# Reordering the prologue of a two-layer attention and FFN kernel, with padding matmuls and a context split moved to GpSimd

## The chip, the core and the metric

The kernel runs on one NeuronCore of a Trainium2 chip. The core has TensorE (PE), VectorE (DVE), ScalarE (ACT), GpSimd (POOL) and SyncE (SP), which here only issues DMAs; each works through its own list of instructions and waits on semaphores for the others. The metric is the device time of one execution in microseconds, lower is better.

## The reference

Sixteen batches of 56 tokens with 128 features attend to a context of 1500 rows each. Cut to what matters:

```
x = x + L0_xattn(layernorm(x), ctx, ctx, Wq, bq, Wk, bk, Wv, bv, Wo)   # 16 heads of 8
x = x + L0_ffn(layernorm(x), w_gate, w_up, w_down)                     # quantised, 384 wide
x = x + L1_xattn(layernorm(x), ctx, ...)                               # slot attention, 3 rounds with a GRU
x = x + L1_ffn(layernorm(x), Wg, Wu, Wd)                               # 8 experts, 512 wide

# L0_xattn
q = (xq @ Wq.T + bq); k = (xk @ Wk.T + bk); v = (xv @ Wv.T + bv)       # split into heads
weights = softmax(q k.T * scale); out = (weights @ v) @ Wo.T
```

The change concerns the first lines only: the first layernorm, the queries, and what the first two batches need before the loop over batches begins.

## The kernel before

**Layout.** Everything is kept with the 128 features on the partitions. `xT` holds all 896 tokens side by side. The context of a batch (128 x 1500 numbers, 750 KB) is loaded into `ctx32` and split into two half-precision parts, `ctx_hi` (a cast) and `ctx_lo` (the difference), so that three half-precision matmuls replace one in single precision. The weights `wk` and `wv` are split in the same way by `split_weights` on DVE: two scaled casts, the scaled bias, two differences.

**The stages of a batch.** `keys` makes 500 columns of keys in three matmuls into PSUM bank `MISC`; ACT casts them to `k_hi` (`k_high`, L711), DVE makes the remainder `k_lo` (`k_low`, L927); there are three such parts, j = 0, 1, 2, and one buffer `k_lo` for all batches. SP copies `k_hi` and `k_lo` with twelve DMAs into `kstack` (`stack`). `values` makes four chunks of values in twelve matmuls (L1495), three times per batch, evacuated by ACT into `v_aug` (L719, L720). GpSimd spreads the queries over heads: `qdiag` (L563) for the maxima, `qstack` (L573) for the scores. `maxima` are 21 units per batch: PE multiplies `qdiag` and `k_hi` into one of two banks (L1508), DVE reduces 500 columns to one (L936). From these the shift of the softmax is taken (`shift_halves`, `shift`, `shift_rows`). Only then can `scores` of that batch go (L1525), twelve steps, each followed by an exponential on ACT (L702) and, every second step, by `weigh` (L1539, L1544).

**Order.** All engines follow an order written out by hand. In the loop `main`, PE interleaves step c of batch b with maxima, keys and values of the next batches; `AHEAD`, `PER_STEP`, `KEYS_AT` and `VALUES_AT` are its tables. Before it comes the prologue. There PE does: means of `xT` (L1461), variance (L1466), first keys (`first_keys`), spread of the reciprocal root over the partitions (L1472), second keys, the queries (L1559), third keys, the 21 maxima of batch 0 with the three value blocks at steps 7, 9 and 11 of `FIRST_STEPS`, the shift, and then keys and first maxima of batch 1. DVE centres (L911), splits the weights (L979 to L984), takes the reciprocal (L915), normalises (L921), takes `q_lo` (L991), casts `ident` (L995) and reduces. ACT casts the first context itself (`context_high`, L724), squares (L692), takes the square root (L697), casts queries (L734) and keys, issues eight of the twelve DMAs that replicate the queries into `q_rep` (L740), and casts the second context. The functions of ACT need tables; a change of table is an instruction of its own.

**Waits that matter.** `keys(b, 0)` waits for `ctx_split` (both parts of the context), for `constants` (the weights' parts) the first time, and for the values before it. The first maximum waits for `qdiag_built`, `k_hi_done` and `ready` at 7, which DVE gives after `ident`. `k_low` of a later batch waits until the DMAs have copied the `k_lo` before it. `scores` waits for the stack, `q_built` and `shift_done`.

## Time and profile before

| | us |
|---|---|
| median of 3 runs | 772.85 (771.12 to 773.10) |
| the profiled execution's own time | 772.33 |
| its span on the core | 770.5 |
| PE busy | 672.9 (87%) |
| DVE busy | 596.2 (77%) |
| ACT busy | 528.6 (69%) |
| GpSimd busy | 444.5 (58%) |

The span runs from the first to the last instruction; 1.8 us of the execution's time lie around it. Times in the text are microseconds from the start of the span. The loop over the batches starts at about 43 us and lasts until about 345 us; the prologue is what comes before it. The page's granted clock is TensorE's clock as a share of 2.4 GHz: it is either 1.00 or 0.50 (1.2 GHz), and a number in between is the mean of a stretch with both.

### The profile page before, as it was taken

The numbers are of one execution on the slowest core, as the hardware profiler recorded it, in microseconds if no ns is written. First come the engines' busy times: TensorE is split into PE (matmuls) and PEld (weight loads), VectorE is DVE, ScalarE is ACT, GpSimd is POOL, SyncE is SP. The second block draws the span as 40 slices with busy tenths as digits, with TensorE's granted clock in tenths as the row PEclk, the third lists the DMA queues.
The fourth block names the chain that finished last, engine by engine and source line by source line (L and its number), as shares of the span: only waits on it lengthen the run. The fifth ranks groups of instructions, "written<-read, shape, count | busy, mean of one in ns | idle before, by whom it ended". The sixth has DMA issues, their size and how long they took to land.

```text
span 770.5 us, 23878 instructions
## 1 busy us (share of the span) xinstructions
PE 672.9 (87%) x8894; PEld 485.5 (63%) x8894; DVE 596.2 (77%) x1122; ACT 528.6 (69%) x1153; POOL 444.5 (58%) x484
## 2 busy tenths in 40 slices
PE   5789999999999999997753868889888688899997
PEld 2257777777777777776531457778888677455553
DVE  3878887887777778888778456888888888858983
ACT  3266776767777677775463398999999984455554
POOL 1667777777777777771100033666776884466564
PEclk8799999999999999999885878999999989999999
DMA  6535444444444444331410501550555431002100
GB/s 191 156 96 174 131 134 121 114 132 140 140 140 130 132 128 133 95 104 20 147 50 0 228 21 64 198 213 28 183 215 186 164 137 63 12 1 83 42 0 25
DMA packets 26864, 86.16 MB, mean 112 GB/s; under 512 B 5844, under 2 KB 7764, under 8 KB 26788
## 3 DMA queue, kind: packets, MB, share of 16 engines
q1 hardware_dynamic: 26408, 84.73, 34.6%
q8 instruction: 46, 0.75, 0.4%
q10 hardware_dynamic: 384, 0.46, 0.2%
q14 instruction: 26, 0.21, 0.1%
HBM read 65.19 MB, written 0.46 MB: 85 GB/s over the span
## 4 chain that ended last, share of the span: by engine, by line
PE 62%; DVE 15%; ACT 15%; issue 3%; SPq 2%; POOL 2%; DMA 1%; DVEq 0%; ACTq 0%; POOLq 0%
PE ps L1508 9%; PE ps L1525 8%; PE ps L1539 8%; ACT c_prob L841 7%; PE ps L1495 5%; PE ps L1818 4%; PE ps L1820 4%; PE ps L1819 4%; PE ps L1766 3%; DVE tile_max L936 3%; PE ps L1484 3%; ACT w0T L841 2%; PE ps L1748 2%; PE ps L1544 2%; ACT merge_w L841 2%
## 5 line engine op out<-in xcount | busy, mean ns | idle before, releaser
L936 DVE TENSOR_REDUCE tile_max<-ps 128x1 f32<-128x500 f32 x336 | 215.2, 675 | 48.8 <-PE ps L1508 48.6
L702 ACT ACTIVATE probs<-ps 125x896 f32<-125x896 f32 x192 | 175.3, 916 | 92.7 <-PE ps L1525 91.8
L1508 PE MATMUL ps<-k_hi,qdiag 128*128 128x500 f16 x336 | 129.6, 387 | 6.7 <-DVE tile_max L936 2.8
L841 ACT ACTIVATE c_prob<-ps,c_bias,row_scale 125x56 f32<-125x56 f32 x384 | 118.8, 547 | 8.1 <-DVE c_bias L1240 8.1
L1525 PE MATMUL ps<-qstack,kstack 98*125 98x224 f16 x768 | 106.3, 261 | 0.4
L631 POOL TENSOR_TENSOR c_prob<-c_prob,c_weight 125x672 f32<-125x672 f32 x32 | 43.1, 1346 | 102.6 <-DVE c_weight L1254 102.5
L1525 PEld LDWEIGHTS ps<-qstack,kstack 98*125 98x125 f16 x768 | 85.8, 136 | 20.9 <-ACT probs L702 2.8
L676 POOL TENSOR_TENSOR ctx_lo<-ctx_hi,ctx_lo 128x448 f16<-128x448 f32 x62 | 64.6, 1042 | 52.1 <-ACT ctx_lo L877 52.1
L1748 PE MATMUL ps<-query_hi,ctx_hi 128*128 128x56 f16 x576 | 54.3, 193 | 29.0 <-ACT c_prob L841 21.0
L1539 PE MATMUL ps<-probs,v_aug 125*32 125x168 f32 x1536 | 74.8, 312 | 3.3 <-ACT probs L702 2.5
L573 POOL TENSOR_TENSOR qstack<-q_rep,slot_mask 96x224 f16<-96x224 f32 (+1 forms) x64 | 33.7, 556 | 74.6 <-PE ps L1525 69.3
L588 POOL TENSOR_TENSOR rows_in<-rows_in 125x768 f32<-125x768 f32 (+2 forms) x96 | 68.9, 717 | 7.5
L1748 PEld LDWEIGHTS ps<-query_hi,ctx_hi 128*128 128x128 f16 x576 | 48.5, 100 | 38.2 <-ACT c_prob L841 23.5
L1818 PE MATMUL ps<-ctx_lo 128*128 128x448 f16 x192 | 67.7, 353 | 3.2 <-DVE ctx_lo L1385 1.6
L1819 PE MATMUL ps<-ctx_lo 128*128 128x448 f16 x192 | 67.7, 352 | 0.0
L1820 PE MATMUL ps<-ctx_lo 128*128 128x448 f16 x192 | 67.7, 352 | 0.0
L872 ACT ACTIVATE ctx_hi<-ps 128x448 f32<-128x448 f32 x64 | 34.8, 543 | 45.5 <-PE ps L1820 45.4
L1539 PEld LDWEIGHTS ps<-probs,v_aug 125*32 125x32 f32 x1536 | 40.2, 109 | 31.8 <-issue 23.8
L1378 DVE SCALAR_TENSOR_TENSOR ctx_hi<-ctx_hi,ps 128x448 f32<-128x448 f32 x64 | 39.0, 614 | 25.7 <-ACT ctx_hi L872 25.4
L558 POOL TENSOR_TENSOR ctx_lo<-ctx,ctx_hi 128x1500 f32 (+1 forms) x16 | 48.6, 3035 | 11.3 <-ACT ctx_hi L724 9.1
L1748 PE MATMUL ps<-query_hi,ctx_lo 128*128 128x56 f16 x576 | 54.0, 192 | 0.0
L1748 PE MATMUL ps<-query_lo,ctx_hi 128*128 128x56 f16 x576 | 54.0, 192 | 0.0
(279 smaller groups left out, 1722.8 us busy)
## 6 DMA issues: line engine op xcount, KB each, us to landing
row_tiles<-in_ctx_rows_wide SPq DMA_DIRECT2D x40, 774.0 KB, 5.7
ctx<-in_ctxT SPq DMA_DIRECT2D x16, 750.0 KB, 5.3
rows_in<-in_ctx_rows SPq DMA_DIRECT2D x16, 750.0 KB
kstack<-k_hi SPq DMA_DIRECT2D x128, 93.8 KB, 2.7
kstack<-k_lo SPq DMA_DIRECT2D x64, 93.8 KB, 2.7
ctx_hi<-in_wg SPq DMA_DIRECT2D x8, 256.0 KB, 2.7
ctx_hi<-in_wu SPq DMA_DIRECT2D x8, 256.0 KB, 3.1
ctx_hi<-in_wd SPq DMA_DIRECT2D x8, 256.0 KB, 3.5
```

The source lines that it names most:

```text
L588: nc.gpsimd.tensor_tensor(a, a, z, ALU.add).then_inc(rows_step, 1)
L676: nc.gpsimd.tensor_tensor(hidden_lo[i], hidden[i], hidden_hi[i], ALU.subtract).then_inc(h_lo_done, 1)
L702: nc.scalar.activation(probs[c % RING_P][0:CH, :].rearrange("p (k w) -> p k w", k=2), score_tile(c)[0:CH], ACT.Exp, scale=float(HD) ** -0. ...
L841: last = nc.scalar.activation(c_prob[n % PROBS][:, c, :], ps[0:CH, 2 * (n % 2) + c // 6, bass.ts(c % 6, TOK)], ACT.Exp, bias=c_bias[n % 2] ...
L936: nc.vector.reduce_max(tile_max[:, u % MAXT, u // MAXT:u // MAXT + 1], ps[:, MAXB + (u + p) % 2, 0:KCOLS], AX.X).then_inc(max_done, 1)
L1508: nc.tensor.matmul(ps[:, MAXB + (u + p) % 2, 0:KCOLS], qdiag[p][:, bass.ts(t, 128)], k_hi[p][:, bass.ts(j, KCOLS)], start=True, stop=True) ...
L1525: last = nc.tensor.matmul(ps[0:CH, 2 * (c % 2) + g // 2, bass.ts(g % 2, GW)], kstack[p][0:STACK_ROWS, g, bass.ts(c, CH)], qstack[p][0:STAC ...
L1539: nc.tensor.matmul(ps[GR * g:GR * g + GR, OUTB, 0:three], v_aug[p][0:CH, of, g, HD:], probs[of % RING_P][0:CH, GW * g:GW * g + three], sta ...
L1748: last = nc.tensor.matmul(ps[:, 2 * (n % 2) + c // 6, bass.ts(c % 6, TOK)], l, r, start=(j == 0), stop=(j == 2))
L1818: nc.tensor.matmul(bank, w1_hi[w][:, at], x_high, start=first, stop=False)
L1819: nc.tensor.matmul(bank, w1_lo[w][:, at], x_high, start=False, stop=False)
L1820: return nc.tensor.matmul(bank, w1_hi[w][:, at], x_low, start=False, stop=last)
```

## The change

1. DVE clears a tile `warm` right at its start, and PE issues matmuls on it whose results nobody reads (`warm_up`, 512 columns each): 10 before the means, 5 between means and variance, 8 between variance and spread.
2. ACT no longer casts the first two contexts; GpSimd does both parts. ACT loads the square root's table at its start instead of at the root.
3. PE does no keys between variance and spread, and only the first keys before the queries; the second come after them, and the third after the first two maxima. DVE splits the weights after the reciprocal instead of before it.
4. GpSimd splits the second context before it spreads the stacked queries, not after.
5. ACT puts the third key's cast between the two groups of four DMAs that replicate the queries.
6. The values of batch 0 come at steps 2, 4 and 6 of the first maxima. `keys(1, 0)` and its cast come at step 9.
7. After the shift, PE does `keys(1, 1)`, then the scores of steps 0 and 1 around the first maximum of batch 1; ACT's first two exponentials follow directly. `main(0, 0)` leaves both out.

The diff, cut to its core:

```diff
-        FIRST_VALUES = {7: 0, 9: 1, 11: 2}
+        FIRST_VALUES = {2: 0, 4: 1, 6: 2}
+        KEY_AHEAD = 9
@@ gpsimd
-                if not (isinstance(b, int) and b < 2):
-                    pool.wait_ge(ctx_loaded[p], landed(b, p, 1))
-                    nc.gpsimd.tensor_copy(ctx_hi[:, b, :], ctx32[:]).then_inc(ctx_split_hi, 1)
+                pool.wait_ge(ctx_loaded[p], landed(b, p, 1))
+                nc.gpsimd.tensor_copy(ctx_hi[:, b, :], ctx32[:]).then_inc(ctx_split_hi, 1)
...
             plain_queries(0, 0)
+            split(1, 1)
             pool.wait_ge(q_rep_loaded, 16 * 3 * GROUPS)
             stacked_queries(0, 0)
-            split(1, 1)
             plain_queries(1, 1)
@@ scalar
-            context_high(0)
+            act.wait_ge(ready, 1)
+            load_table(ACT.Sqrt)
             act.wait_ge(ready, 3)
             layernorm_sd(0)
             act.wait_ge(constants, 1)
             k_high(0, 0, 0)
-            k_high(0, 0, 1)
...
-            k_high(0, 0, 2)
+            k_high(0, 0, 1)
             act.wait_ge(q_hi_done, 2)
             for r in range(2):
+                if r:
+                    k_high(0, 0, 2)
                 for g in range(GROUPS):
                     nc.scalar.dma_start(q_rep[GR * r:GR * (r + 1), g, :], q_hi[GR * g:GR * (g + 1), :]).then_inc(q_rep_loaded, 16)
-            context_high(1)
             for c in range(NCH):
                 if c in FIRST_VALUES:
                     v_evacuate(0, 0, FIRST_VALUES[c])
+                if c == KEY_AHEAD:
+                    k_high(1, 1, 0)
                 if c == NCH - 1:
                     load_table(ACT.Exp)
-            k_high(1, 1, 0)
             k_high(1, 1, 1)
+            exp(0, 0)
+            exp(0, 1)
@@ vector
             nc.vector.memset(eps_ln[:], LN_EPS).then_inc(ready, 1)
+            nc.vector.memset(warm[:], 0.0).then_inc(magic_ready, 1)
...
-            layernorm(0, split_weights, lambda: k_low(0, 0, 0))
-            k_low(0, 0, 1)
+            layernorm(0, None, split_weights)
+            k_low(0, 0, 0)
...
-            k_low(0, 0, 2)
+            k_low(0, 0, 1)
             dve.wait_ge(params, PARAMS)
             nc.vector.tensor_copy(ident[:], ident32[:]).then_inc(ready, 1)
             for c in range(NCH):
                 maxima(0, 0, step_units(FIRST_STEPS, c))
+                if c == 0:
+                    k_low(0, 0, 2)
...
+            k_low(1, 1, 0)
             shift_rows(0, 0)
-            k_low(1, 1, 0)
-            maxima(1, 1, range(1))
             k_low(1, 1, 1)
-            maxima(1, 1, range(1, UNITS_AHEAD))
+            maxima(1, 1, range(UNITS_AHEAD))
@@ tensor
+            def warm_up(n):
+
+                for _ in range(n):
+                    nc.tensor.matmul(ps[:, MAXB + 1, 0:512], warm[:, 0:128], warm[:], start=True, stop=True)
+
+            pe.wait_ge(magic_ready, 1)
+            warm_up(10)
             pe.wait_ge(first_params, 16 * len(first_list))
-            layernorm(0, None, first_keys)
-            keys(0, 1)
+            layernorm(0, lambda: warm_up(5), lambda: warm_up(8))
+            pe.wait_ge(constants, 1)
+            keys(0, 0)
...
-            keys(0, 2)
+            keys(0, 1)
...
                 maxima(0, 0, second)
+                if c == 0:
+                    keys(0, 2)
+                if c == KEY_AHEAD:
+                    keys(1, 0)
                 if c == NCH - 1:
                     shift(0, 0)
-            keys(1, 0)
+            keys(1, 1)
+            scores(0, 0, 0)
             maxima(1, 1, range(1))
-            keys(1, 1)
+            scores(0, 0, 1)
             maxima(1, 1, range(1, UNITS_AHEAD))
```

On DVE, from the centring to the first maxima (`out_raw` is the memory of the early weights, of the normalised x and of `q_lo`). Before:

```order
L911 TENSOR_TENSOR probs<-xT,ps 128x448 [waits ln_mean,first_params]
L911 TENSOR_TENSOR probs<-xT,ps 128x448 [waits ln_mean]
L979 TENSOR_SCALAR wk_hi<-out_raw 128x128 [waits k_params]
L984 SCALAR_TENSOR_TENSOR wv_lo<-out_raw,wv_hi 128x128
L915 RECIPROCAL rstd<-sd 128x224 [waits ln_sd]
L927 SCALAR_TENSOR_TENSOR k_lo<-ps,bk_scaled,k_hi 128x500 [waits k_hi_done]
L921 TENSOR_TENSOR out_raw<-probs,ps 128x448 [waits ln_spread] x2
L995 CAST ident<-ident 128x128 [waits params]
L936 TENSOR_REDUCE tile_max<-ps 128x1 [waits max_ready] x21
```

Now:

```order
L913 TENSOR_TENSOR probs<-xT,ps 128x448 [waits ln_mean,first_params]
L913 TENSOR_TENSOR probs<-xT,ps 128x448 [waits ln_mean]
L917 RECIPROCAL rstd<-sd 128x224 [waits ln_sd]
L982 TENSOR_SCALAR wk_hi<-out_raw 128x128 [waits k_params]
L987 SCALAR_TENSOR_TENSOR wv_lo<-out_raw,wv_hi 128x128
L923 TENSOR_TENSOR out_raw<-probs,ps 128x448 [waits ln_spread] x2
L998 CAST ident<-ident 128x128 [waits params]
L938 TENSOR_REDUCE tile_max<-ps 128x1 [waits max_ready] x2
L929 SCALAR_TENSOR_TENSOR k_lo<-ps,bk_scaled,k_hi 128x500 [waits k_hi_done]
L938 TENSOR_REDUCE tile_max<-ps 128x1 [waits max_ready] x19
```

The five instructions of the splits (two shown) moved behind the reciprocal, and one `k_lo` went in among the reductions.

On GpSimd, from its start to the spreading of the second batch's queries. Before:

```order
L558 TENSOR_TENSOR ctx_lo<-ctx,ctx_hi 128x1500 [waits ctx_split_hi]
L563 TENSOR_TENSOR qdiag<-q_hi,head_mask 128x896 [waits q_hi_done,params]
L573 TENSOR_TENSOR qstack<-q_rep,slot_mask 96x224 [waits q_rep_loaded]
L573 TENSOR_TENSOR qstack<-q_rep,slot_mask 96x224 x3
L558 TENSOR_TENSOR ctx_lo<-ctx,ctx_hi 128x1500 [waits ctx_split_hi]
```

Now:

```order
L557 CAST ctx_hi<-ctx 128x1500 [waits ctx_loaded0]
L559 TENSOR_TENSOR ctx_lo<-ctx,ctx_hi 128x1500 [waits ctx_split_hi]
L564 TENSOR_TENSOR qdiag<-q_hi,head_mask 128x896 [waits q_hi_done,params]
L557 CAST ctx_hi<-ctx 128x1500 [waits ctx_loaded1]
L559 TENSOR_TENSOR ctx_lo<-ctx,ctx_hi 128x1500 [waits ctx_split_hi]
L574 TENSOR_TENSOR qstack<-q_rep,slot_mask 96x224 [waits q_rep_loaded]
```

Both casts came to this engine, and the second context follows `qdiag` directly.

On PE, from the shift of batch 0 into the loop. Before:

```order
L1515 MATMUL ps<-ident,neg_pair 2x128 [waits pair_done]
L1484 MATMUL ps<-ctx_hi,wk_hi 128x500 [waits v_done,ctx_split]
L1508 MATMUL ps<-k_hi,qdiag 128x500 [waits k_hi_done,qdiag_built,max_done]
L1484 MATMUL ps<-ctx_hi,wk_hi 128x500 [waits k_lo_done]
L1508 MATMUL ps<-k_hi,qdiag 128x500 [waits shift_done,max_done]
L1525 MATMUL ps<-qstack,kstack 125x224 [waits shift_done,q_built,stack_loaded0]
L1508 MATMUL ps<-k_hi,qdiag 128x500 [waits max_done] x2
L1525 MATMUL ps<-qstack,kstack 125x224 x4
```

Now:

```order
L1488 MATMUL ps<-ctx_hi,wk_hi 128x500 [waits v_done,ctx_split]
L1512 MATMUL ps<-k_hi,qdiag 128x500 [waits max_done]
L1519 MATMUL ps<-ident,neg_pair 2x128 [waits pair_done]
L1488 MATMUL ps<-ctx_hi,wk_hi 128x500 [waits k_lo_done]
L1529 MATMUL ps<-qstack,kstack 125x224 [waits shift_done,q_built,stack_loaded0]
L1512 MATMUL ps<-k_hi,qdiag 128x500 [waits k_hi_done,qdiag_built,max_done]
L1529 MATMUL ps<-qstack,kstack 125x224 x4
L1512 MATMUL ps<-k_hi,qdiag 128x500 [waits shift_done,max_done]
```

The first keys of batch 1 moved ahead of the last maximum and the shift, and the first two scores ahead of all but one of batch 1's maxima.

## Rows read from the trace of the kernel before

**Rows 1.** Busy time by stretch: stretch, its length, each engine's busy time, PEclk, DMA

```profile
100.00:200.00 100.00, 97.94 (x1512) 71.89 (x1511) 80.93 (x142) 70.89 (x102) 74.49 (x70) 1.00 0.45 131
```

**Rows 2.** The chain that ended last, in order of time: start, us, what

```profile
9.93 3.03 POOL ctx_lo L558
...
14.50 3.04 PE ps L1472 x8
...
20.27 0.82 PE ps L1484 x3
...
21.11 0.69 ACT k_hi L711
21.82 0.74 DVE k_lo L927
...
32.56 1.28 PE ps L1495 x12
...
36.00 0.71 PE ps L1495 x12
...
39.06 1.28 ACT L684
```

**Rows 3.** Busy time by stretch, in the prologue; the third number from the right is PEclk

```profile
5.00:8.60 3.60, 3.29 (x4) 1.18 (x4) 0.70 (x2) 0.19 (x1) 0.00 (x0) 1.00 0.95 298
...
14.30:17.60 3.30, 3.30 (x10) 2.71 (x10) 1.38 (x3) 0.68 (x1) 0.00 (x0) 0.50 0.65 250
...
25.30:32.00 6.70, 5.83 (x11) 0.98 (x11) 6.59 (x11) 1.44 (x1) 4.00 (x5) 0.50 0.73 179
```

**Rows 4.** Matmuls of two lines: duration in ns min/median/max, first and last start

```profile
L1461 PE MATMUL ps<-xT,ones_mean x4: 891/954/1116, 5.2 to 7.6; 128*128 128x448 f32 x4
...
L1559 PE MATMUL ps<-out_raw x4: 539/539/540, 18.6 to 19.7; 128*128 128x448 f32 x4
```

**Rows 5.** Timeline, 8 to 23 us: start, us, engine, line, instruction, idle before

```profile
8.41 1.44 ACT L724 CAST ctx_hi<-ctx 128x1500 f16<-128x1500 f32 x1 [6.39 <-DMA ctx<-in_ctxT]
...
9.06 0.22 DVE L979 TENSOR_SCALAR wk_hi<-out_raw 128x128 f16<-128x128 f32 x1
...
9.76 1.04 ACT L692 ACTIVATE probs<-probs 128x448 f32<-128x448 f32 x2
...
10.81 1.28 ACT L697 ACT_TABLE_LOAD   x1
...
12.58 1.55 DVE L915 RECIPROCAL rstd<-sd 128x224 f32<-128x224 f32 x1 [2.64 <-ACT sd L697]
...
17.58 0.62 DVE L921 TENSOR_TENSOR out_raw<-probs,ps 128x448 f32<-128x448 f32 x1 [0.87 <-PE ps L1472]
...
19.52 1.39 ACT L734 ACTIVATE q_hi<-ps,bias_qkv 128x448 f16<-128x448 f32 x2
...
21.05 1.69 POOL L563 TENSOR_TENSOR qdiag<-q_hi,head_mask 128x896 f16<-128x896 f16 x1 [8.10 <-ACT q_hi L734]
...
21.12 5.28 ACTq L740 DMA_DIRECT2D q_rep<-q_hi  x8
...
22.48 0.34 DVE L995 CAST ident<-ident 128x128 f16<-128x128 f32 x1
```

**Rows 6.** Timelines of DVE and of GpSimd in a later stage, 638 to 640 us

```profile
638.79 1.02 DVE L1338 TENSOR_SCALAR rs_y<-rs_var 128x112 int32<-128x112 int32 x1
...
638.05 1.69 POOL L631 TENSOR_TENSOR merge_w<-merge_w,c_weight 125x672 f32<-125x672 f32 x1 [1.21 <-DVE c_weight L1254]
639.82 1.49 POOL L641 TENSOR_SCALAR ctx_lo<-ctx_hi 128x512 f16<-128x512 f32 x1
```

**Rows 7.** Timeline of DVE: the 21 reductions of batch 0

```profile
23.30 9.98 DVE L936 TENSOR_REDUCE tile_max<-ps 128x1 f32<-128x500 f32 x15 [0.48 <-PE ps L1508]
34.29 3.91 DVE L936 TENSOR_REDUCE tile_max<-ps 128x1 f32<-128x500 f32 x6 [1.02 <-PE ps L1508]
```

**Rows 8.** Timeline: the first and the third exponential of batch 0 on ACT

```profile
43.60 0.92 ACT L702 ACTIVATE probs<-ps 125x896 f32<-125x896 f32 x1
...
47.72 0.92 ACT L702 ACTIVATE probs<-ps 125x896 f32<-125x896 f32 x1
```

More of the change, by code:

```diff
@@ L720, in v_evacuate @@
                 nc.scalar.activation(dst[:, :, 0:HD], src[:, :, GR - HD:], ACT.Copy, scale=1.0 / W_SCALE).then_inc(v_done, 1)
-            def context_high(b):
-                act.wait_ge(ctx_loaded[b], 16)
-                nc.scalar.copy(ctx_hi[:, b, :], ctx32[:]).then_inc(ctx_split_hi, 1)
-            context_high(0)
+            act.wait_ge(ready, 1)
+            load_table(ACT.Sqrt)
             act.wait_ge(ready, 3)
```

20 lines of the change are left out of this document (10 added, 10 removed).

## The prediction

> **What bounds the kernel now.** I read the busy time by stretch first. Between 100 and 200 us, in the loop over the batches, PE is busy 97.94 us of 100 [rows 1]: this stage is a queue of PE work, so whatever comes before it moves its end by the same amount, and a head start is neither lost nor multiplied. The change touches only what lies before that loop, the first 46 us. Every gain has to be found there, and I follow it to the third exponential of batch 0 (47.72 us), after which both kernels issue the same instructions in the same order.
>
> Second, the chain of waits. It comes through the first context's load, ACT's cast, GpSimd's subtraction up to 12.96 us [rows 2], the queries, 21 reductions on DVE, and a table load of 1.28 us on ACT in front of the second batch's first key. Third, the granted clock of TensorE [rows 3]. It is 0.50 from 14.3 to 17.6 and from 25.3 to 32.0, the second being a stretch in which PE issues one matmul per reduction. The record says 1.00 from 5.0 to 8.6, but there the durations contradict it: the mean's matmuls take 954 ns a record and the queries', of the same shape, 539 ns [rows 4]. So the means also ran at 1.2 GHz, and the engine was idle before them.
>
> **Part 1, normalisation.** Before, ACT casts the context (1.44 us), then squares from 9.76, then loads a table from 10.81 (1.28 us), and the reciprocal starts at 12.58 [rows 5]. Afterwards GpSimd does the cast, which costs it about the same, so its subtraction still ends near 12.96. The table is loaded during the first DMA wait, the squares follow the centring at once, and the reciprocal starts between 9.3 and 10.7, depending on how early the 10 + 5 + 8 padding matmuls lift the clock. Even the late end leaves the reciprocal's end (1.55 us long) before 12.96. So the early chain is not worth its own 2 to 3 us: it runs into GpSimd.
>
> It runs into it twice. `keys(0, 0)`, which now stands ahead of the queries on PE, needs `ctx_lo`, as it did. And DVE's splits of the weights, five instructions of which the first starts at 9.06 and takes 0.22 us [rows 5], move from a time at which GpSimd had not begun to one in which it subtracts. The row at 638.79 shows what this does: an elementwise DVE instruction on 112 columns takes 1.02 us, beginning while GpSimd works from 638.05 for 1.69 us, and ends 0.07 us behind it, just as GpSimd's next begins at 639.82 [rows 6]. I take it that the splits wait until 12.96 and then take their 0.9 us (9.06 to about 9.94 before), to 13.9. The Trainium skill, "SBUF — State Buffer", section "Who interferes with whom", says that a VectorE instruction with two SBUF inputs, or in a two-port mode, and a GpSimd instruction that reads SBUF exclude each other for the whole instruction. By that rule, which speaks against this order of the splits, the trace agrees; without it term 1 would be the better end of its bounds, below.
>
> The two halves of the normalised x (0.62 us each, the last at 17.58 before [rows 5]) then end at 15.1, where they ended at 18.20. From there to the end of the second `q_hi` it was 2.71 us (to 20.91), of which some 0.3 was PE finishing key matmuls; now 2.4, to 17.5. **Term 1: -3.4 us.** The normalised halves count here because they queue behind the splits on DVE. Bounds: if the splits are not held up, `keys(0, 0)` is what remains and this is 1.2 us better (-4.6); if the queries run at 1.2 GHz (their four records at 0.95 instead of 0.54 [rows 4], less overlap), 1.0 worse.
>
> From `q_hi` to the first reduction it was 2.39 us (20.91 to 23.30): `qdiag` on GpSimd beside key cast, `k_lo` and `ident` [rows 5, 7]. The same instructions stand there now, with the second key in the third's place: 0. But `ident` took 0.34 us and ended as `qdiag` did, 22.8: it too was held by GpSimd. Now GpSimd goes straight on with the second context's cast and subtraction (1.43 and 3.02 us). `ident` is due 0.2 us before `qdiag` ends, and gets its turn between the two. Bounds: 0 to +4.5, on which the rivals below turn.
>
> **Part 2, the maxima.** 21 reductions took 14.9 us, 23.30 to 38.20: 9.98 us for 15, 3.91 for 6, and one stall of 1.02 [rows 7]. The third key is now inside. DVE has `k_lo` there (0.74, some 0.7 pipelined [rows 2]), and waits about 0.5 for it, because ACT issues four of its eight query DMAs (5.28 us for eight [rows 5]) before it gets to that key's cast. **Term 2: +1.2 us.** The row on ACT's second context cast leaves for GpSimd, which has the slack.
>
> The stall comes from `values`: its twelve matmuls take 1.28 us at half clock against 0.71 at full [rows 2]; with one matmul for the next reduction behind them that is more than the one reduction that DVE has in hand. Before, the first block met the half clock and the other two the full one. Now the blocks stand at steps 2, 4 and 6, just after 5 us in which PE has almost nothing (two maxima, a key), which is what it did before the fall at 25.3. I expect the first block surely and the second about as likely as not at half clock: 1.5 stalls for one. **Term 3: +0.5 us** (0 stalls -1.0, 3 stalls +2.0). The last reduction then ends at 36.5 instead of 38.2.
>
> **Part 3, into the loop.** Call the last reduction's end E. Before, shift, `keys(1, 0)`, table load and its key cast followed, the first exponential came at E + 5.4 and the third at E + 9.5 [rows 8]. Now `keys(1, 0)` and its cast lie before E and the table load beside shift and shift copy. After E: shift values 0.6, `k_lo` 0.74, shift copy 0.63, `keys(1, 1)` from E + 1.45 for 0.82, its cast 0.69, so the first exponential at E + 3.0, a gain of 2.4. This doesn't last: the second batch's seven reductions before the third exponential begin after `k_lo` at E + 3.75 and take 7 x 0.665 = 4.7 us, so its scores come behind the seventh matmul at about E + 7.4, and the third exponential at E + 8.0. **Term 4: -1.5 us.** What is late next is DVE, not ACT. The copies of the second batch's key are ready with `k_lo`, nearly as much sooner. If the clock is at half again here (PE is sparse in the last seven reductions), the key's matmuls, the scores and the first loop steps cost 1.0 to 1.2 more; I give that 4 in 10. **Term 5: +0.4 us.**
>
> The memset of the padding's operand (under 0.5 us of DVE) lies in the DMA wait, and the 10 padding matmuls end before or up to 0.3 us after the data arrive: nothing, as that path has room up to 12.96.
>
> **The sum:** -3.4 + 1.2 + 0.5 - 1.5 + 0.4 = -2.8 us on the profiled execution's 772.33 us, which is 0.5 us under the median of 772.85: 769.5 us.
>
> **Rivals.**
> (a) Full clock throughout: no stall of the maxima and none in the loop's start, -1.5 - 0.4 on the sum: -4.7, 767.6 us. For it: the padding keeps PE dense up to 10.7. Against it: nothing pads PE after the queries.
> (b) The splits are not held: -4.0, 768.3 us. Against it is the row at 638.79.
> (c) `ident` arrives after GpSimd has gone on to the second context's cast and waits for that alone: +1.4, so 770.9 us. It needs a second key 0.2 us late, which half clock in the queries gives.
> (d) Slower: the same, but GpSimd passes from cast to subtraction without letting DVE in, so that `ident`, and with it the first maximum (which waits for `ready`), comes 4.5 us later. It decides from the moment that `ident` is issued behind `qdiag`'s end: -2.8 + 4.5 = +1.7, 774.0 us. Against it: at 639.8 DVE did get in between two.
> (e) The padding, all zeros, does not lift the clock. Then 23 matmuls stand in front for nothing: the variance waits for five (at 0.42 each), the spread for part of eight and itself runs at half clock (3.04 us [rows 2]), and `q_hi` ends at 20.1 to 23. With the middle of these, 20.7, term 1 is about 0 and the whole -0.2 to +0.6: 772.3 us. The Trainium skill, "TensorE: Matmul & The Clock Gate", Part 1, says that activity releases the throttle, and that all-zero operands do not trip another, current-driven limiter; by it padding of zeros should count. No row here has such matmuls.
>
> **How the numbers follow.** The forecast (-1.6 to -4.0) has 0.56, (a) 0.12, (b) 0.08, (c) 0.10, (d) 0.05, (e) 0.09. Leaving out (d) and the far end of (a), the range is 767.8 to 772.2 us. About 0.3%, 2.3 us, is what a measurement of this kernel can tell from no change. The forecast's middle lies only 0.5 beyond it, so two thirds of it count as faster, all of (a) and (b), and little else: faster 0.57. Slower by over 0.3% needs (d) with a second stall, or a worse (e): 0.05. The same: 0.38.
>
> **What would show it.** In the profile after: the variance's reciprocal well before 12.9, but the first split of the weights lasting until GpSimd's subtraction ends (if it takes 0.22, term 1 is larger); the first reduction near 19.9; `ident` ending within 0.1 us of `qdiag`; a gap of DVE near 1.0 us behind the first `values`, perhaps the second; the last reduction at 36 to 37; the third exponential 8 us behind it, and the rest of the execution as before, shifted. The prediction is wrong if the subtraction of the first context no longer ends near 13, if the maxima run without stalls, or if the clock in later stages falls elsewhere by chance and moves the end by more than the prologue does.

## The result, and the profile after the change

The changed kernel takes 770.66 us (median of 22 executions, 765.50 to 773.86), the kernel before 772.91 us beside it (22 executions): the ratio is 0.996, 95% interval 0.9945 to 0.9974. The ratios in this document are the estimates on record from the fast executions, not quotients of the medians beside them (here that would be 0.9971). The profiled execution took 771.68 us with a span of 769.8 us. Lines have moved a little against the rows of before: L702 is now L703, L936 is L938, L1484 is L1488, L1508 is L1512.

The prologue first. GpSimd's timeline (start, us, engine, line, instruction, idle before and its releaser):

```profile
9.02 1.43 POOL L557 CAST ctx_hi<-ctx 128x1500 f16<-128x1500 f32 x1 [8.20 <-DMA ctx<-in_ctxT]
10.54 3.03 POOL L559 TENSOR_TENSOR ctx_lo<-ctx,ctx_hi 128x1500 f16<-128x1500 f32 x1
...
19.65 1.43 POOL L557 CAST ctx_hi<-ctx 128x1500 f16<-128x1500 f32 x1
```

DVE's timeline of the same kernel, 9 to 21 us:

```profile
9.73 1.55 DVE L917 RECIPROCAL rstd<-sd 128x224 f32<-128x224 f32 x1 [1.80 <-ACT sd L698]
11.20 2.45 DVE L982 TENSOR_SCALAR wk_hi<-out_raw 128x128 f16<-128x128 f32 x1
...
14.23 1.15 DVE L923 TENSOR_TENSOR out_raw<-probs,ps 128x448 f32<-128x448 f32 x2
...
19.24 0.55 DVE L998 CAST ident<-ident 128x128 f16<-128x128 f32 x1
20.27 1.26 DVE L938 TENSOR_REDUCE tile_max<-ps 128x1 f32<-128x500 f32 x2 [0.48 <-PE ps L1512]
```

PE's timeline, the means, the spread and the first key:

```profile
5.50 1.77 PE L1465 MATMUL ps<-xT,ones_mean 128*128 128x448 f32 x4 [0.48 <-DMA spread<-in_spread]
...
11.34 1.78 PE L1476 MATMUL ps<-rstd,spread 128*128 128x224 f32 x8 [0.32 <-DVE rstd L917]
14.37 0.39 PE L1488 MATMUL ps<-ctx_hi,wk_hi 128*128 128x500 f16 x1 [1.25 <-DVE wv_lo L987]
```

Against [rows 2, 5]: the four means take 1.77 us instead of 3.29 and the spread 1.78 instead of 3.25 (3.04 on the chain of [rows 2]), so both run at 2.4 GHz. The reciprocal starts at 9.73 instead of 12.58. Then the first split lasts 2.45 us instead of 0.22 and ends at 13.65, 0.08 us behind GpSimd's subtraction. `ident` ends at 19.79, between `qdiag` and GpSimd's next instruction.

The maxima and the way into the loop, DVE's timeline:

```profile
21.82 0.74 DVE L929 SCALAR_TENSOR_TENSOR k_lo<-ps,bk_scaled,k_hi 128x500 f16<-128x500 f32 x1 [0.29 <-ACT k_hi L712]
22.48 2.04 DVE L938 TENSOR_REDUCE tile_max<-ps 128x1 f32<-128x500 f32 x3
25.54 2.64 DVE L938 TENSOR_REDUCE tile_max<-ps 128x1 f32<-128x500 f32 x4 [1.02 <-PE ps L1512]
28.77 2.43 DVE L938 TENSOR_REDUCE tile_max<-ps 128x1 f32<-128x500 f32 x4 [0.59 <-PE ps L1512]
31.41 4.19 DVE L938 TENSOR_REDUCE tile_max<-ps 128x1 f32<-128x500 f32 x7 [0.21 <-PE ps L1512]
36.38 0.68 DVE L938 TENSOR_REDUCE tile_max<-ps 128x1 f32<-128x500 f32 x1 [0.77 <-PE ps L1512]
```

The first and the third exponential, ACT's timeline:

```profile
40.79 0.92 ACT L703 ACTIVATE probs<-ps 125x896 f32<-125x896 f32 x1
...
45.72 0.92 ACT L703 ACTIVATE probs<-ps 125x896 f32<-125x896 f32 x1
```

Busy time by stretch; the third number from the right is the granted clock:

```profile
22.00:28.00 6.00, 4.62 (x26) 2.70 (x26) 4.76 (x8) 0.66 (x2) 2.18 (x1) 0.50 0.79 201
28.00:30.00 2.00, 1.32 (x10) 0.55 (x9) 1.41 (x4) 0.66 (x2) 1.79 (x4) 0.97 0.53 133
...
36.00:40.00 4.00, 2.60 (x13) 1.29 (x13) 2.48 (x6) 2.12 (x3) 3.92 (x3) 0.50 0.00 0
```

Where [rows 7] have one stall of DVE behind `values`, there are four, 2.59 us together: one at half clock (1.02), one in whose block of values the clock rises (0.59), one at full (0.21), and one of 0.77 us ahead of the last reduction, which is `keys(1, 0)`: its three matmuls take 0.37, 0.58 and 0.62 us, as the clock falls in the middle of them. The last reduction ends at 37.06 instead of 38.20. The clock is at 0.50 again from 36 to 40 us, and the third exponential comes at 45.72 instead of 47.72 [rows 8]: 2.00 us sooner, though the first context landed 0.6 us later in this execution (9.02 against 8.41).

Those 2.00 us don't arrive at the end. The copies of the shifted queries mark each batch on DVE (before, then after):

```profile
102.29 0.63 DVE L953 COPY qstack<-ps 2x896 f16<-2x896 f16 x1 [0.64 <-PE ps L1515]
...
143.59 0.63 DVE L953 COPY qstack<-ps 2x896 f16<-2x896 f16 x1 [0.64 <-PE ps L1515]
```

```profile
100.23 0.63 DVE L955 COPY qstack<-ps 2x896 f16<-2x896 f16 x1 [0.64 <-PE ps L1519]
...
141.70 0.63 DVE L955 COPY qstack<-ps 2x896 f16<-2x896 f16 x1 [0.65 <-PE ps L1519]
```

Two batches, one turn of the loop, take 41.30 us before and 41.47 after. Of the five turns from here to 307.40 us four take 41.46 to 41.48 us, where before all take 41.24 to 41.30; at the last copy (349.27 against 348.07) the lead is 1.20 us. On PE, after the change, the first scores of these four turns stand behind an idle of 0.24 to 0.32 us for which the profile names no releaser (issue); before has none there:

```profile
123.75 0.59 PE L1529 MATMUL ps<-qstack,kstack 98*125 98x224 f16 x4 [0.24 <-issue]
```

This table gives such marks for every profile, so that what was drawn by chance (when the context lands) stands apart from what the kernel does. Context: start of its first cast. Queries and maxima: end of the second `q_hi` and start of the first reduction, behind the context. Block: from the first reduction to the end of the 21st. Start: from there to the third exponential. Loop: from there to the last (sixteenth) copy of the shifted queries. Rest: from there to the span's end. All in us; the ratio is that to before. `after_again` is the changed kernel once more: it was run to see whether the loss per turn belonged to one execution. It doesn't: most turns take 41.45 to 41.50 us again.

| kernel | context | queries | maxima | block | start | loop | rest | ratio (95%) |
|---|---|---|---|---|---|---|---|---|
| before | 8.41 | 12.50 | 14.89 | 14.90 | 9.52 | 301.55 | 421.23 | |
| changed | 9.02 | 8.85 | 11.25 | 16.79 | 8.66 | 302.35 | 421.73 | 0.996 (0.9945 to 0.9974) |
| after_again | 8.77 | 8.85 | 11.24 | 16.20 | 7.67 | 302.39 | 420.63 | 0.9936 (0.9909 to 0.9964) |
| splits_early | 8.51 | 11.75 | 14.14 | 14.57 | 7.67 | 302.41 | 425.40 | 1.0009 (0.9984 to 1.0034) |
| splits_early_again | 9.05 | 12.81 | 15.21 | 16.78 | 8.67 | 302.47 | 421.62 | |
| no_padding | 9.12 | 10.66 | 13.05 | 16.21 | 7.67 | 301.50 | 420.95 | 0.9964 (0.9933 to 0.9995) |
| values_later | 9.23 | 8.84 | 11.24 | 16.54 | 7.67 | 302.55 | 420.27 | 0.9958 (0.9928 to 0.9988) |
| pad_maxima | 9.47 | 10.09 | 12.48 | 14.62 | 7.67 | 302.31 | 417.75 | 0.9893 (0.9839 to 0.9946) |
| pad_maxima_again | 9.82 | 8.86 | 11.25 | 14.62 | 8.77 | 302.01 | 417.33 | 0.9923 (0.9899 to 0.9947) |
| pad_both | 8.57 | 8.84 | 11.24 | 14.62 | 7.66 | 301.75 | 421.06 | 0.9907 (0.9884 to 0.993) |
| shift_code | 7.90 | 9.08 | 11.60 | 15.39 | 7.67 | 301.57 | 420.57 | 0.9923 (0.9901 to 0.9945) |
| ident_late | 8.76 | 8.91 | 12.67 | 16.28 | 7.67 | 302.52 | 417.50 | |
| queries_first | 8.75 | 10.46 | 14.23 | 15.83 | 7.67 | 302.49 | 420.13 | 0.9975 (0.9954 to 0.9997) |
| loop_start_old | 7.79 | 8.85 | 11.24 | 14.52 | 12.67 | 302.35 | 422.63 | 0.998 (0.9953 to 1.0006) |

### The profile page after: what moved, and what is told of

It is laid out like the page before. It is cut to its first block, busy times and chain, and to the rows that moved or that the text cites. A ratio compares the mean times of both kernels' runs of the same rounds, so it can differ in the third digit from the quotient of the medians.

```text
span 769.8 us, 23925 instructions
## 1 busy us (share of the span) xinstructions
PE 675.6 (88%) x8917; PEld 487.0 (63%) x8917; DVE 597.5 (78%) x1123; ACT 525.1 (68%) x1151; POOL 447.1 (58%) x486
## 4 chain that ended last, share of the span: by engine, by line
PE 62%; DVE 16%; ACT 14%; issue 3%; SPq 2%; POOL 1%; DMA 1%; DVEq 0%; ACTq 0%; POOLq 0%
PE ps L1512 10%; PE ps L1529 9%; PE ps L1543 8%; ACT c_prob L843 7%; PE ps L1499 5%; PE ps L1832 4%; PE ps L1834 4%; PE ps L1833 4%; PE ps L1780 4%; PE ps L1488 3%; DVE tile_max L938 3%; ACT w0T L843 2%; PE ps L1762 2%; PE ps L1548 2%; ACT merge_w L843 2%
## 5 line engine op out<-in xcount | busy, mean ns | idle before, releaser
L938 DVE TENSOR_REDUCE tile_max<-ps 128x1 f32<-128x500 f32 x336 | 214.5, 675 | 51.3 <-PE ps L1512 51.0
L703 ACT ACTIVATE probs<-ps 125x896 f32<-125x896 f32 x192 | 175.3, 916 | 93.0 <-PE ps L1529 92.1
L1512 PE MATMUL ps<-k_hi,qdiag 128*128 128x500 f16 x336 | 128.4, 384 | 6.5 <-DVE tile_max L938 4.4
L1529 PEld LDWEIGHTS ps<-qstack,kstack 98*125 98x125 f16 x768 | 86.5, 137 | 22.3 <-ACT probs L703 3.7
L1241 DVE TENSOR_REDUCE ps<-ps 125x12 f32<-125x672 f32 x48 | 41.2, 859 | 15.9 <-PE ps L1762 15.8
```

Source lines behind the costliest of these rows:

```text
L703: nc.scalar.activation(probs[c % RING_P][0:CH, :].rearrange("p (k w) -> p k w", k=2), score_tile(c)[0:CH], ACT.Exp, scale=float(HD) ** -0. ...
L938: nc.vector.reduce_max(tile_max[:, u % MAXT, u // MAXT:u // MAXT + 1], ps[:, MAXB + (u + p) % 2, 0:KCOLS], AX.X).then_inc(max_done, 1)
L1512: nc.tensor.matmul(ps[:, MAXB + (u + p) % 2, 0:KCOLS], qdiag[p][:, bass.ts(t, 128)], k_hi[p][:, bass.ts(j, KCOLS)], start=True, stop=True) ...
L1529: last = nc.tensor.matmul(ps[0:CH, 2 * (c % 2) + g // 2, bass.ts(g % 2, GW)], kstack[p][0:STACK_ROWS, g, bass.ts(c, CH)], qstack[p][0:STAC ...
```

## The experiments

**Are the splits held by GpSimd, and can they get away from it?**

```
-            layernorm(0, None, split_weights)
+            layernorm(0, split_weights, None)
```

> The changed kernel, with the splits of the weights put back ahead of the variance's reciprocal on VectorE, where they stood before; all else stays. Theory (the splits were held for GpSimd's 3.03 us subtraction of the first context, the first split taking 2.45 us instead of 0.22): the splits now run between the centring and the reciprocal, beside GpSimd's cast rather than its subtraction, and take 0.9 us in all; the reciprocal may be held in their place but it is one instruction and its successors pass through PE; keys(0, 0) waits for GpSimd's subtraction alone, and the second q_hi ends 0.6 to 1.0 us sooner after the context has landed (9.0 instead of 9.7 us), third exponential and end -0.6 to -1.0 us. Rival (the lock only hands its wait to the next instruction on VectorE: the reciprocal or the normalised halves are held until the subtraction ends instead): second q_hi as in the changed kernel or up to 1.5 us later, end 0 to +1.5 us.

> The variant splits_early once more. Theory A (its 3.5 us over the changed kernel come from a fall of the clock at 362 to 369 us, by which its output projection and scores take 2.4 us longer, and more behind 400 us; the program makes it, as the ten executions at 774 us suggest): granted clock under 0.8 between 360 and 370 us again, end near 774. Theory B (that fall is a matter of chance): 1.00 between 360 and 370 us, end 770 to 772. The first splits of the weights take over 2 us in either, held by GpSimd's subtraction.

Measured: 774.19 us (10 executions; before 772.53), and 775.61 us for the second profile's execution. My theory got the cause right (GpSimd holds the splits) and the remedy wrong. DVE in the second profile, and GpSimd beside it:

```profile
9.80 0.76 DVE L982 TENSOR_SCALAR wk_hi<-out_raw 128x128 f16<-128x128 f32 x1 [1.50 <-DMA bias_qkv<-in_bias_qkv]
...
10.73 3.00 DVE L986 SCALAR_TENSOR_TENSOR wk_lo<-out_raw,wk_hi 128x128 f16<-128x128 f32 x1
...
13.86 1.54 DVE L917 RECIPROCAL rstd<-sd 128x224 f32<-128x224 f32 x1
```

```profile
10.56 3.02 POOL L559 TENSOR_TENSOR ctx_lo<-ctx,ctx_hi 128x1500 f16<-128x1500 f32 x1
```

The weights land at 9.80 us, when GpSimd is already in its cast. The first split ends 0.08 us behind that cast, the fourth waits out the whole subtraction (3.00 us instead of 0.29). From the context's landing to 13.6 us there is no gap of GpSimd's for them, and now the reciprocal queues behind them: it starts at 13.86 instead of 9.73, and the queries end 2.9 and 4.0 us later than in the changed kernel. That is the rival of the first expectation, at a higher price than its 1.5 us; 1.5 us of the 4.0 are the spread, which ran at half clock in the second profile (3.26 us instead of 1.78). Before, ACT did the cast, so GpSimd was still idle when the splits ran. By the rule of the Trainium skill, "SBUF — State Buffer", section "Who interferes with whom" (a VectorE instruction with two SBUF inputs or in a two-port mode and a GpSimd instruction that reads SBUF exclude each other), the traces agree: in eleven profiles a split starts before the subtraction's end and lasts until then, 0.6 to 3.0 us; in the first one of pad_maxima it starts behind it and takes 0.16 us. The reciprocal, with one input, ran beside GpSimd in its usual 1.55 us.

Of the second expectation, theory B holds for the clock: it was granted in full between 360 and 370 us this time, where the first profile had 0.70 (360 to 365) and 0.62 (365 to 370). Its time doesn't hold: 775.61 us instead of 770 to 772. In the first profile the late queries were repaid in the maxima (block 14.57 us, full clock) and lost again behind 345 us (rest of 425.40); in the second they weren't repaid. So the fall at 362 us isn't made by the program. That the slow median of ten comes from the prologue is likely, not shown: of the two profiles only the second is slow for that reason.

**What is the padding worth?**

```
-            warm_up(10)
+            warm_up(0)
...
-            layernorm(0, lambda: warm_up(5), lambda: warm_up(8))
+            layernorm(0)
```

> The changed kernel without its 23 matmuls of zeros; all else stays. Theory (the padding lifts the clock, as the means' 443 ns a record against 954 before suggests): means at 0.95 us a record, the variance later by about 1.5 us, still ahead of GpSimd's subtraction; spread and queries wholly or partly at half clock, second q_hi 0.5 to 1.5 us later after the context has landed (10.2 to 11.2 instead of 9.7 us), and the stalls behind the values as in the changed kernel: end +0.5 to +1.5 us. Rival (the path is pinned by GpSimd's subtraction and the held splits, so the clock ahead of it is worth nothing): second q_hi within 0.3 us of the changed kernel's and end within 0.3 us.

Measured: 770.74 us, ratio 0.9964, the same as the changed kernel's. PE's timeline:

```profile
5.89 3.32 PE L1465 MATMUL ps<-xT,ones_mean 128*128 128x448 f32 x4 [5.89 <-DMA spread<-in_spread]
...
13.27 3.35 PE L1476 MATMUL ps<-rstd,spread 128*128 128x224 f32 x8 [2.15 <-DVE rstd L917]
```

Matmuls of zeros do lift the clock: without them the means and the spread run at half of it, and the queries end 1.81 us later (10.66 against 8.85). The theory's part on the clock holds; its +0.5 to +1.5 us at the end don't come, and part of the reason is in the table: the loop is 0.85 us shorter than with the padding. Padding in the prologue is also no certain remedy: of the ten profiles with 10 matmuls of zeros at the start, the means took 1.77 us in seven, 2.47 in one and 3.35 in two (splits_early, queries_first). That led to the next run.

**Why do the turns of the loop take longer?**

```
-            warm_up(10)
+            warm_up(14)
```

> The changed kernel with 14 instead of 10 matmuls of zeros at the start, in the wait for the first DMAs; all else stays. It moves TensorE's instructions of the loop over the batches by four matmuls. In the loop the changed kernel and the two variants with as many matmuls ahead of the loop (splits_early, values_later) show an idle of 0.24 to 0.26 us put down to issue at the start of each turn, and lose 0.17 us per turn against before, 1.2 us in all; before, no_padding (23 fewer) and pad_maxima (20 more) don't. Theory (it depends on where the loop lies in the instruction memory, hence on the number of matmuls ahead): with four more the idle may stay or go, but it is the same in every turn, and it stands apart from the clock and from the prologue's times. Rival (it depends on the phase in which the loop is entered or on what another engine does in it): the idle stands as in the changed kernel, with copies of the shifted queries 41.4 us apart per turn. In both the prologue is that of the changed kernel within 0.5 us.

Measured: 767.41 us (2 executions, before 774.08). PE's first turn and DVE's copies:

```profile
120.50 0.59 PE L1529 MATMUL ps<-qstack,kstack 98*125 98x224 f16 x4 [0.19 <-issue]
```

```profile
138.47 0.63 DVE L955 COPY qstack<-ps 2x896 f16<-2x896 f16 x1 [0.64 <-PE ps L1519]
...
179.71 0.63 DVE L955 COPY qstack<-ps 2x896 f16<-2x896 f16 x1 [0.64 <-PE ps L1519]
```

The idle stands in the first turn alone; the next takes 41.24 us, and the loop 301.57 us as before, with the same instructions in it. So the rival (the idle stays as it was) is refuted, and the theory holds but for its "the same in every turn". (The expectation's 1.2 us in all is too much: the loop's difference is 0.80.) All eight profiles of kernels with 23 matmuls of zeros have the longer loop (302.35 to 302.55), those with 0 (before, no_padding) and 27 don't (301.50 to 301.57), and none of the three with 41 has the idle (their loops take 301.75 to 302.31 us, by longer first batches, which I haven't followed up). What is shown is that the number of matmuls ahead of the loop matters. Why is argued: what differs is where the loop's instructions lie. A load of instructions from memory isn't it: the trace lists packets of kind "instruction" on the DMA queues, and none of them moves between 130 and 330 us, where three of the four idles stand (206.5, 248.0 and 289.5 us). A phase in which the loop is entered is unlikely, since the third exponential comes between 43.88 and 49.71 us in the eight and the idle is there in all; and the other engines' programs are the same in the changed kernel and in shift_code.

**The values' place in the maxima.**

```
-        FIRST_VALUES = {2: 0, 4: 1, 6: 2}
+        FIRST_VALUES = {5: 0, 7: 1, 9: 2}
```

> The changed kernel with the three blocks of the first batch's values at steps 5, 7 and 9 of the maxima instead of 2, 4 and 6; all else stays. Theory (a block stalls VectorE by what its twelve matmuls take at half clock over at full, and what counts is how dense the blocks follow): the first block meets the half clock (stall near 1.0), the second and third as now (0.6 and 0.2), but the denser end lifts the clock for keys(1, 0), so that the 0.77 us stall ahead of the last reduction goes; last reduction 0 to 0.8 us sooner, third exponential up to 1.5 us sooner, end -0.3 to -1.5 us. Rival (the position doesn't matter, the stalls only move): the stalls' sum stays within 0.3 us of 2.59 and the end within 0.3 us.

Measured: 769.52 us, ratio 0.9958. DVE's timeline:

```profile
29.40 2.44 DVE L938 TENSOR_REDUCE tile_max<-ps 128x1 f32<-128x500 f32 x4 [1.00 <-PE ps L1512]
...
36.33 0.68 DVE L938 TENSOR_REDUCE tile_max<-ps 128x1 f32<-128x500 f32 x1 [0.95 <-PE ps L1512]
```

PE's timeline, ahead of the last reduction:

```profile
34.29 0.37 PE L1512 MATMUL ps<-k_hi,qdiag 128*128 128x500 f16 x1
35.29 0.37 PE L1488 MATMUL ps<-ctx_hi,wk_hi 128*128 128x500 f16 x1 [0.63 <-ACT v_aug L721]
```

The stalls are 1.00, 0.21, 0.21 and 0.95 us, 2.37 in all, instead of 2.59 and, in the second profile of the changed kernel, 2.01. By its number the rival holds, but the position does matter. The first block met the half clock again, because the clock fell later in this execution (at 25.8 us instead of 21.3). The last stall isn't one of the clock, which was granted in full from 29.2 us on: the edit puts the third block of values and `keys(1, 0)` into the same step, and the key's matmuls wait 0.63 us until ACT has evacuated that block. So this run doesn't test what a denser end is worth; one with the key a step later would. The end can't tell either: 0.9958 and 0.996 are the same within their intervals.

**The clock in the maxima.** Matmuls of zeros into a bank that is free there (18 more; the expectation's 20 is a slip of mine):

```
+            warm_up(7, 2)
             pe.wait_ge(ready, 7)
...
+                if c == 1:
+                    warm_up(3, 2)
+                if 7 <= c < KEY_AHEAD:
+                    warm_up(2, 2)
...
+                if c == KEY_AHEAD + 1:
+                    warm_up(4, 2)
```

> The changed kernel with 20 more matmuls of zeros, into a bank of PSUM that nothing else uses then: 7 ahead of the first maximum, 3 behind step 1, 2 behind each of steps 7 and 8, 4 behind step 10. Theory (the half clock is what makes the stalls of 1.02, 0.59, 0.21 and 0.77 us in the maxima and costs some 0.7 us at the loop's start): granted clock 1.00 through 20 to 42 us, stalls together under 0.8 us instead of 2.59, third exponential 8.0 instead of 8.66 us behind the last reduction; end -2 to -3 us. Rival (the padding stands in front of the maxima's own matmuls and only turns one stall into another, or the clock falls all the same): stalls together over 2 us and end -0.5 to +1.0 us.

> The variant pad_maxima once more, for its time and a second profile (it has 18 more matmuls of zeros than the changed kernel, not 20 as its first expectation says). Theory (full clock through the maxima and no idle in the loop's turns, 2.2 us and 1.2 us): stalls together under 1 us, third exponential 7.7 us behind the last reduction, ratio to before 0.990 to 0.995. Rival (its -6 us were for the most part a good draw behind 345 us): the maxima as said, ratio 0.995 to 0.998.

and, with 14 at the start, 6 ahead of the first maximum and 2 at each of the other places:

> Like pad_maxima with as many matmuls of zeros in all (41), spread otherwise: 14 instead of 10 at the start, so that they reach to 6.5 us and the wait for the spread's DMA (it landed between 5.2 and 7.4 us) finds TensorE busy; 6 ahead of the first maximum, 2 behind steps 1, 7, 8 and 10. Theory (a late spread DMA lets the clock fall before the means, which cost pad_maxima 0.7 and splits_early 1.6 us there; a longer padding closes it): means at 1.77 us for four records, second q_hi 8.9 us behind the context, maxima at full clock: 0 to -1.2 us against pad_maxima. Rival (fewer matmuls of zeros in the maxima let the clock fall there): stalls over 2 us, +1 to +2 us.

Measured: pad_maxima 766.33 and 766.07 us (before 772.53 and 772.92), pad_both 765.59 us, where the changed kernel beside it took 768.43. Stretches and reductions of pad_both:

```profile
22.00:28.00 6.00, 3.88 (x32) 2.16 (x32) 5.57 (x11) 1.32 (x4) 1.73 (x1) 1.00 0.75 181
...
36.00:40.00 4.00, 2.79 (x16) 1.32 (x14) 3.05 (x6) 2.29 (x3) 3.92 (x3) 1.00 0.01 2
```

```profile
24.07 2.43 DVE L938 TENSOR_REDUCE tile_max<-ps 128x1 f32<-128x500 f32 x4 [0.21 <-PE ps L1512]
...
33.75 0.68 DVE L938 TENSOR_REDUCE tile_max<-ps 128x1 f32<-128x500 f32 x1 [0.15 <-PE ps L1512]
```

For the maxima the theory holds in all three profiles: granted clock 1.00, stalls 0.21 three times and 0.15, a block of 14.62 us instead of 16.79 and 16.20. The full clock came without padding too, by itself, in splits_early and loop_start_old (blocks of 14.57 and 14.52 us), so part of this could be a draw; three out of three, and three medians below the changed kernel's two, speak against it. At the loop's start the theory holds in two of three: in pad_maxima_again the clock fell at 42 us, behind the last padding, and the start took 8.77 us. The reductions also come closer, 2.43 us for four where 9.98 for 15 [rows 7] stood mostly at half clock. One reduction lasts 0.67 to 0.68 us in both; but at full clock the next starts 0.59 us behind it, in before at half clock 0.67 to 0.70. There TensorE's record for a unit lasts 0.60 us instead of 0.38, and it waits for the bank that a reduction frees; so the likely reading is that the reductions wait for TensorE, in waits too short for the view to list. Of pad_maxima's 6 us over before, though, 3.5 to 3.9 lie behind 345 us (rest of 417.75 and 417.33 against 421.23), which pad_both's profile doesn't have: that part can't be put down to the padding. In pad_maxima the wait for the spread's DMA let the clock fall before the means once (2.47 us for four instead of 1.77); with 14 at the start they took 1.67 us in both kernels that have them. Against pad_maxima pad_both gained 0.5 us by the medians, which is within what was forecast and within the noise. pad_both is the version to keep: ratio 0.9907, 95% interval 0.9884 to 0.993, which lies wholly below the changed kernel's first interval and overlaps its second (0.9909 to 0.9964).

**Does `ident` wait once or twice?** A reciprocal of 112 columns that nothing reads delays it:

```
             dve.wait_ge(params, PARAMS)
+            nc.vector.reciprocal(rstd[:, 0:WIDE[0] // 4], sd[:, 0:WIDE[0] // 4])
             nc.vector.tensor_copy(ident[:], ident32[:]).then_inc(ready, 1)
```

> The changed kernel with one more instruction on VectorE (a reciprocal of 112 columns that nothing reads, about 0.8 us) just ahead of the cast of ident; all else stays. The cast now arrives some 0.4 us after GpSimd has gone on from qdiag to the cast of the second context (19.65 to 21.08 in the changed kernel). Theory of one wait (rival (c) of the prediction: VectorE gets in at the next boundary between two GpSimd instructions): ident ends as that cast does, near 21.2, and the first reduction starts 1.4 us later than in the changed kernel. Theory of two waits (rival (d): GpSimd keeps the port through cast and subtraction): ident ends near 24.2, the first reduction is 4.4 us later. No lock at all: +0.8.

Measured: DVE, and GpSimd's instruction behind the cast that ended at 20.87:

```profile
19.79 1.17 DVE L999 CAST ident<-ident 128x128 f16<-128x128 f32 x1
```

```profile
20.95 3.02 POOL L559 TENSOR_TENSOR ctx_lo<-ctx,ctx_hi 128x1500 f16<-128x1500 f32 x1
```

Where nothing holds it, as in queries_first, this cast takes 0.22 us. Here `ident` ends at 20.96, as the cast has ended (20.87) and the subtraction begins, and the maxima start 1.42 to 1.43 us later behind the context (12.67 against 11.25 and 11.24). One wait: the mechanism of (c), at its price of 1.4 us; (d) is refuted. The single execution took 767.19 us, no slower than the changed kernel: its rest is 417.50 us.

**Are the queries the path, or the keys?** The splits and `ident` go behind the normalised halves, the queries ahead of the first key on PE and ACT:

```
-            layernorm(0, None, split_weights)
-            k_low(0, 0, 0)
+            layernorm(0)
+            split_weights()
...
-            pe.wait_ge(constants, 1)
-            keys(0, 0)
             pe.wait_ge(ln_out, 2)
...
+            pe.wait_ge(constants, 1)
+            keys(0, 0)
             keys(0, 1)
```

> The changed kernel with the splits of the weights moved behind the two halves of the normalised x on VectorE (and ident's cast right behind them), the queries ahead of the first key on TensorE and ScalarE; all else stays. Theory (what term 1 stands on: the queries were late only because they queued behind splits that waited for GpSimd): the normalised halves end 0.8 us behind the spread's matmuls, the second q_hi ends 1.0 to 1.7 us sooner after the context has landed (7.2 to 7.9 us behind it instead of 8.85), the splits take 0.9 us as GpSimd has ended, the first reduction is 0.7 to 1.3 us sooner, the end -0.5 to -1.3 us. Rival (the key path, splits to first key to k_lo, is as long: what the queries gain the keys lose): first reduction within 0.3 us, end within 0.3 us. Second rival (clock: a head start given back by a longer half clock in the maxima, as splits_early's 2.4 us were repaid there): the last reduction within 0.3 us though the first is sooner.

Measured: 771.00 us, ratio 0.9975. DVE's timeline:

```profile
16.63 0.22 DVE L982 TENSOR_SCALAR wk_hi<-out_raw 128x128 f16<-128x128 f32 x1
...
22.32 0.74 DVE L929 SCALAR_TENSOR_TENSOR k_lo<-ps,bk_scaled,k_hi 128x500 f16<-128x500 f32 x1 [1.61 <-ACT k_hi L712]
```

Behind GpSimd's end a split takes 0.22 us again. But `k_lo` of the second key is now what the first reduction waits for: 3.77 us behind the queries instead of 2.40. In this execution the means ran at half clock (3.35 us), which spoils the comparison behind the context; counted from the spread's end (16.05; 13.12 in the changed kernel) the first reduction comes 6.93 us later instead of 7.15. The first rival holds for the first reduction: what the queries gain, the keys lose (0.22 us are left). The ends, 0.9975 and 0.996, can't be told apart.

**The way into the loop.** The prediction's part 3 undone: `keys(1, 0)` behind the shift, the first two scores and the order of `k_lo` and shift as before. PE's part of the edit (ACT and DVE follow it):

```
-                if c == KEY_AHEAD:
-                    keys(1, 0)
...
-            keys(1, 1)
-            scores(0, 0, 0)
+            keys(1, 0)
             maxima(1, 1, range(1))
-            scores(0, 0, 1)
+            keys(1, 1)
             maxima(1, 1, range(1, UNITS_AHEAD))
```

> The changed kernel with the way into the loop put back as before: the second batch's first key behind the shift instead of at step 9 of the maxima, the table of the exponential and the scores of the first two steps in the old order. Theory (term 4 of the prediction: this part is worth 1.5 us at equal clock): third exponential 9.5 us behind the last reduction at full clock, 10.5 at half, instead of 7.67 and 8.66; the stall of 0.77 us ahead of the last reduction is gone, as keys(1, 0) no longer stands there: together +1.0 to +1.5 us at the loop's start. Rival (the part is worth nothing, as VectorE's seven reductions of the second batch pace the start either way): third exponential within 0.3 us of the changed kernel's.

Measured: 773.00 us, ratio 0.998. A stretch and the third exponential:

```profile
33.00:44.00 11.00, 8.25 (x28) 3.74 (x29) 6.29 (x13) 2.70 (x4) 10.20 (x6) 0.50 0.22 75
```

```profile
46.22 0.92 ACT L703 ACTIVATE probs<-ps 125x896 f32<-125x896 f32 x1 [0.30 <-PE ps L1527]
```

The stall ahead of the last reduction is gone, and the block takes 14.52 us at full clock. Then the clock is at half for all of 11 us, and the third exponential comes 12.67 us behind them: 3.15 us more than before had at full clock (9.52), 4.0 to 5.0 more than the changed kernel. The rival is refuted, and the theory was right in its direction and too small: it had 10.5 us at half clock. The old order costs 1.85 us more at full clock (9.52 in before against 7.67), and 4.0 more at half (12.67 against 8.66); that it has more of TensorE's work for a half clock to stretch is my reading, not tested.

## Why the prediction was right, and where it was not

Forecast 769.5 us, range 767.8 to 772.2, measured 770.66. Some of this nearness is luck. The sum of -2.8 us was set on one profiled execution (772.33); set on the median of 772.85 it gives 770.05. Behind the context the two profiles of the changed kernel gained 2.61 and 4.20 us up to the third exponential, on average 0.6 more than forecast, and the loop, which the sum put at nothing, gave 0.8 back: two errors of opposite sign. By the medians 2.25 us are left, by the ratio 3.1. By its own steps:

- **Term 1** (-3.4 us): -3.65 behind the context in both profiles of the changed kernel. The early chain ran into GpSimd twice as described, the first split ended 0.08 us behind the subtraction. Rival (b) is refuted, and its gain is not to be had by moving the splits.
- **From `q_hi` to the first reduction** (0): 2.40 us against 2.39. `ident` got its turn between two GpSimd instructions. Rivals (c) and (d) didn't come about.
- **Terms 2 and 3** (+1.2 and +0.5): the block grew by 1.89 and by 1.30 us against the forecast 1.7. The third key cost 0.95 (from 21.53 to 22.48), so term 2 was 0.25 too large. Term 3 was mis-sized: 1.57 and 0.99 us of stalls over before's 1.02. I had one and a half blocks of values at half clock, but not `keys(1, 0)` in front of the last reduction (0.77 us when the clock falls there, 0.15 when not). What balanced it is that the reductions of before lay further apart at half clock (13.89 us for the 21 without the stall, 13.24 in the changed kernel).
- **Term 4** (-1.5): -1.85 at full clock (7.67 against 9.52). DVE's seven reductions are what is late next, as said. **Term 5** (0.4 of 1.0 to 1.2 us): the half clock came in one profile of two and cost 0.99.
- **To the third exponential** the sum was -2.8. Measured behind the context: -2.61 and -4.20 us.
- **The step that failed** is the first one: that a head start is neither lost nor multiplied, and that the two kernels are equal behind it. The loop takes 0.80 and 0.84 us longer with the same instructions, when 23 matmuls more stand ahead of it; that their place in the code does it is the likely reason, not a shown one. Without this the change would be worth that much more, as shift_code suggests. Nothing in the rows of before could give its size, but it should have stood among what could make the prediction wrong.
- **Rival (e)** is refuted: zeros lift the clock. (Its time was off by itself: the middle of -0.2 to +0.6 on 772.33 is 772.5, not 772.3.) **Rival (a)**, full clock throughout, didn't come by itself; pad_both made it, where block and start take 22.3 us together; (a) had 15.1 + 8.0 = 23.1.

Three things stay open. Why the number of matmuls ahead of the loop changes its turns. The rest behind 345 us takes 417.3 to 425.4 us; the granted clock there falls at other places in each profile, two profiles of one kernel differ by 0.4, 1.1 and 3.8 us, and no run tells what decides it. And why the changed kernel's ratio was 0.996 in one set of executions and 0.9936 in another: the intervals overlap, so it may be chance.

## What to carry to other kernels

- Where a short chain runs beside GpSimd, list which of its VectorE instructions read SBUF twice or are plain casts and scalings (here they waited 0.6 to 3.0 us for one GpSimd instruction), and look for a gap of GpSimd's in which they can run; if there is none, put them where nothing queues behind them.
- In a stretch in which TensorE has one matmul per step of another engine, try matmuls of zeros behind some of the steps: here they kept the clock at full in three profiles of three, and none of the orders of the real work that were tried did so reliably. Measure each place: the padding of the prologue alone lifted the clock there and didn't change the end (770.74 us without it, 770.66 with it).
- When a loop of unchanged instructions takes longer after an edit ahead of it, look for an idle put down to issue at its first instruction, and try a few instructions more or fewer ahead of it before giving up the edit.
- When an edit moves a stage, check which other stage then stands in the same step: values_later kept its stall of about 1 us, but for a new reason.

## What the runs showed of the chip that I had not expected

- With 23 matmuls more ahead of a loop most of its turns of 41.3 us take 0.2 us longer, and with four further ones only the first turn (41.40 us) does.
- A VectorE instruction held by GpSimd gets its turn between two GpSimd instructions that follow each other within 0.1 us (seen at 19.65, at 20.95 in ident_late, at 10.56 in splits_early_again and, before, at 639.8); in none of these cases did one instruction wait for two of GpSimd's.
- The first context's cast starts anywhere between 7.79 and 9.82 us in the 14 profiles, and two profiles of one kernel differ by 0.25 to 0.54, so prologues are compared from that mark and not from zero.
- At half clock VectorE's reductions start 0.67 to 0.70 us apart instead of 0.59, though each lasts 0.67 to 0.68 in both and the profile lists no wait between them.
